# Query and key projection from a split context tile, with the last weighing ahead of the denominator columns

## The chip, the cores and the metric

The kernel runs on one core of one Trainium2 chip. The metric is the device time in microseconds of one execution over the whole input; lower is better. All inputs lie in the chip's memory at the start, and the output is written there.

## The reference

The input `x` holds 32 batches of 128 rows and 1024 columns; `ctx_4096` (the context) has the same shape. Four layers follow each other, each added to x. `_layernorm` is over the last axis.

```python
x = x + _L0_xattn_ref(_layernorm(x), ctx, ...)   # attention over the 1024 columns
x = x + _L0_ffn_ref(_layernorm(x), ...)          # routed product with sign(weight)
x = x + _L1_xattn_ref(_layernorm(x), ctx, ...)   # attention over the 128 context rows
x = x + _L1_ffn_ref(_layernorm(x), ...)          # routed low-rank product
```

The change touches the first layer. There C = 128, T = 1024 and the width of queries and keys is 64:

```python
q = jnp.einsum('dc,bct->btd', Wq, init) + bq     # init is the context
k = jnp.einsum('dc,bct->bdt', Wk, init) + bk[None, :, None]
R = jnp.einsum('btd,bds->bts', q, k)
attention = jax.nn.softmax(R, axis=-1)
v = jnp.einsum('oc,bct->bto', Wv, x) + bv
out = jnp.einsum('bts,bsc->bct', attention, v)
```

## The kernel before

**Trips.** After a set-up block that loads and prepares the weights, all engines run the function `body(k, prepare, attend, chain)` for k = 0 to 33 (`iterations`, L634). Trip k works on three batches at once: it prepares batch b = k (projection, transposed context, values), attends batch a = k - 1 (the first layer's attention over 1024 x 1024 scores) and runs the chain of the three other layers on batch c = k - 2. Trips 2 to 31 do all three; they are the steady state. Trips 0 and 1 lack the later stages, and trips 32 and 33 do not prepare.

**Order.** Every engine has its instructions in a hand-written order, and semaphores tie the engines together. Nothing is reordered by a scheduler: an engine that waits holds up all that stands behind it. SyncE issues the DMAs.

**Two kinds of matmul.** Tiles of type F32 are multiplied in full precision; the hardware records show two matmuls for each such product. Tiles of type F32R hold rounded values, and the records show one matmul each. To keep precision with rounded operands the kernel splits many tiles into a rounded part (`_hi`) and the rest (`_lo`), and adds three products: hi with hi, lo with hi, hi with lo.

**The inner loop.** In each trip the loop over s = 0 to 7 makes one block of scores ahead (`key_scores`), takes the exponent on ScalarE (`prob`), rounds it on ScalarE (`p_hi`), forms the rest on VectorE (`p_lo`), adds to the sum on VectorE (`p_sum`), and multiplies with the values on TensorE (`weigh_values`, six rounded matmuls into `acc`). Steps of the chain are laid in between.

**Its last step, s = 7, on TensorE.** First come the two products of the third layer's attention, `att` half 1 into `shared[1]` (L1338) and half 0 into `shared[0]` (L1340), with `attnT` and `c_val` in full precision. Then the projection of the next batch (L1345): `wqkT`, which holds both weights, times the context tile `c_in`, two halves of 512 columns, into `scores[0]`. Then the sums of the denominators with narrow matmuls (L1352), the eight transposes of `c_in` into `shared` (L1144), and `denominator_columns` (L1221), two transposes of `den_wide`. Then `weigh_values` for s = 7. After the loop eight transposes of `den_inv` (L1372) follow, the transposes of `xn_3` (L1144, the tile is called `p_sum` in the rows since it shares its memory), the values (L1150) and the low-rank product (L1396).

**What VectorE does beside it.** Behind `p_lo` and `p_sum` of s = 6 it writes `kwT` half 0 (`keys_turned`, L932), the reciprocal `r_inv` (L1047), and `p_lo` of s = 7 (L1010). Then it adds the two att halves to `res` (L1052), half 1 first, takes the statistics of `res` (L867 to L875), copies `den_wide` (L906), forms the rest of q (L1068, half 0), the reciprocal `den_inv` (L911), the rest of q (half 1), and `cT_lo` in two halves (L1076). The reciprocal waits for `denominator_columns` on TensorE. The `xn_3` transposes reuse `shared`, half by half, and so wait for the matching half of `cT_lo`; the `c_in` transposes reuse it too, and wait for both halves of `res`.

**What ScalarE does beside it.** It evicts q and k from the projection (L822, L824), then `cT_hi` (L831, L833), `xn_3` (L737) and the denominators (L743).

## Time and profile before

| | before |
|---|---|
| median of 3 runs | 2154.66 us (2151.1 to 2155.81) |
| profiled execution | 2152.07 us |
| its span, first to last instruction | 2150.1 us |
| TensorE matmul busy | 2123.1 us, 99% |
| TensorE weight load busy | 1667.2 us, 78% |
| VectorE busy | 1852.7 us, 86% |
| ScalarE busy | 1160.4 us, 54% |
| mean granted TensorE clock | 0.997 of full speed |

The times of the table are medians of separate executions; the profile is one more execution, 2.6 us below the median. The busy share of an engine says how full it is, not whether another waits for it. The ends of matmuls are modelled, so consecutive matmul rows overlap; the distance from one start to the next (the pitch) is what an instruction costs. The rows of the weight load (PEld) show short waits that the matmul rows hide. For VectorE and ScalarE too, the pitch is a little shorter than the duration of a row.

### The profile page before, as it was taken

The numbers are of one execution on the slowest core, as the hardware profiler recorded it, in microseconds if no ns is written. First come the engines' busy times: TensorE is split into PE (matmuls) and PEld (weight loads), VectorE is DVE, ScalarE is ACT, GpSimd is POOL, SyncE is SP. The second block draws the span as 40 slices with busy tenths as digits, with TensorE's granted clock in tenths as the row PEclk, the third lists the DMA queues.
The fourth block names the chain that finished last, engine by engine and source line by source line (L and its number), as shares of the span: only waits on it lengthen the run. The fifth ranks groups of instructions, "written<-read, shape, count | busy, mean of one in ns | idle before, by whom it ended". The sixth has DMA issues, their size and how long they took to land.

```text
span 2150.1 us, 35721 instructions
## 1 busy us (share of the span) xinstructions
PE 2123.1 (99%) x11503; PEld 1667.2 (78%) x11503; DVE 1852.7 (86%) x3098; ACT 1160.4 (54%) x1721; POOL 264.2 (12%) x306
## 2 busy tenths in 40 slices
PE   9989999999999999999999999999999999999998
PEld 7867777777877777787777777877777787777777
DVE  8268899988888998888899988888998888898984
ACT  4145555655555556555555665555556555555651
POOL 0010111111111111111111111111111111111100
PEclk9999999999999999999999999999999999999999
DMA  6454443233343333334343233343333334343210
GB/s 217 143 157 128 126 129 110 89 113 127 127 137 117 124 100 96 128 118 137 122 131 108 88 117 127 127 137 117 123 97 97 127 122 137 119 135 105 90 50 30
DMA packets 110874, 254.03 MB, mean 118 GB/s; under 512 B 12976, under 2 KB 14272, under 8 KB 110848
## 3 DMA queue, kind: packets, MB, share of 16 engines
q1 hardware_dynamic: 110848, 253.69, 36.8%
q8 instruction: 16, 0.26, 0.1%
q14 instruction: 10, 0.08, 0.0%
HBM read 215.89 MB, written 20.97 MB: 110 GB/s over the span
## 4 chain that ended last, share of the span: by engine, by line
PE 92%; DVE 1%; ACT 1%; issue 1%; POOL 0%; DVEq 0%; POOLq 0%; ACTq 0%
PE acc L1215 17%; PE shared L1144 7%; PE scores L1164 6%; PE acc L1175 6%; PE shared L1189 6%; PE acc L1178 6%; PE acc L1176 6%; PE shared L1190 6%; PE scores L1204 5%; PE scores L1203 5%; PE shared L1396 3%; PE shared L1322 3%; PE scores L1150 3%; PE scores L1345 3%; PE scores L1352 1%; PE shared L1263 1%
## 5 line engine op out<-in xcount | busy, mean ns | idle before, releaser
L1010 DVE TENSOR_TENSOR p_lo<-prob,p_hi 128x1024 fp32r<-128x1024 f32 x256 | 312.3, 1220 | 103.7 <-ACT p_hi L800 85.9
L793 ACT ACTIVATE prob<-scores 128x1024 f32<-128x1024 f32 x256 | 260.7, 1018 | 236.7 <-PE scores L1204 185.5
L885 DVE TENSOR_REDUCE neg_max<-scores 128x1 f32<-128x1024 f32 x256 | 306.9, 1220 | 42.0 <-PE scores L1164 35.1
L704 POOL TENSOR_TENSOR rstd<-var_eps,minus_half 128x1 f32<-128x1 f32 x128 | 126.9, 991 | 1739.9 <-DVE var_eps L875 1739.9
L800 ACT ACTIVATE p_hi<-prob 128x1024 fp32r<-128x1024 f32 x256 | 271.2, 1059 | 42.7 <-PE acc L1215 38.5
L1175 PE MATMUL acc<-m_hi,cT_hi 128*128 128x512 f32 x512 | 217.6, 425 | 0.9 <-DVE x L919 0.9
L1189 PE MATMUL shared<-signT,y_hi 128*128 128x512 f32 x512 | 204.4, 399 | 0.0
L1203 PE MATMUL scores<-q_hl,k_hh 128*128 128x512 f32 x512 | 201.5, 394 | 1.9 <-DVE q_m L992 1.5
L1178 PE MATMUL acc<-m_ring,cT_hi 128*128 128x512 f32 x512 | 203.2, 397 | 0.0
L1176 PE MATMUL acc<-m_hi,cT_lo 128*128 128x512 f32 x512 | 202.5, 396 | 0.0
L1204 PE MATMUL scores<-q_m,k_l 128*128 128x512 f32 x512 | 202.2, 395 | 0.0
L1190 PE MATMUL shared<-signT,y_lo 128*128 128x512 f32 x512 | 201.8, 394 | 0.0
L1018 DVE TENSOR_TENSOR p_sum<-p_sum,prob 128x1024 f32<-128x1024 f32 x160 | 195.0, 1219 | 0.0
L1215 PE MATMUL acc<-p_hi,v_hi 128*128 128x512 f32 x512 | 170.8, 415 | 4.4 <-DVE p_lo L1010 3.9
L1164 PE MATMUL scores<-k_hh,q_hl 128*128 128x512 f32 x512 | 165.2, 404 | 0.3 <-issue 0.3
L1215 PE MATMUL acc<-p_hi,v_lo 128*128 128x512 f32 x512 | 160.9, 395 | 0.0
L1215 PE MATMUL acc<-p_lo,v_hi 128*128 128x512 f32 x512 | 160.8, 395 | 0.0
L1203 PEld LDWEIGHTS scores<-q_hl,k_hh 128*128 128x128 f32 x512 | 96.1, 188 | 25.7 <-issue 1.6
L1164 PEld LDWEIGHTS scores<-k_hh,q_hl 128*128 128x128 f32 x512 | 91.5, 188 | 31.1 <-issue 7.0
L1178 PEld LDWEIGHTS acc<-m_ring,cT_hi 128*128 128x128 f32 x512 | 96.4, 188 | 23.1
L1215 PEld LDWEIGHTS acc<-p_lo,v_hi 128*128 128x128 f32 x512 | 96.0, 188 | 23.4
L1204 PEld LDWEIGHTS scores<-q_m,k_l 128*128 128x128 f32 x512 | 96.1, 188 | 23.1
(222 smaller groups left out, 4214.3 us busy)
## 6 DMA issues: line engine op xcount, KB each, us to landing
m_ring<-m_low SPq DMA_DIRECT2D x512, 256.0 KB, 3.1
c_in<-in_ctx SPq DMA_DIRECT2D x32, 512.0 KB, 3.4
xn<-in_x SPq DMA_DIRECT2D x32, 512.0 KB, 4.2
x<-in_x SPq DMA_DIRECT2D x32, 512.0 KB, 3.3
c_val<-in_ctx SPq DMA_DIRECT2D x32, 512.0 KB, 3.8
out_x<-oscale SPq DMA_DIRECT2D x32, 512.0 KB, 3.0
q_m<-q_hl SPq DMA_DIRECT2D x32, 256.0 KB, 3.1
k_hh<-k_hh SPq DMA_DIRECT2D x32, 256.0 KB, 3.5
```

The lines of the kernel that those rows point to most:

```text
L800: nc.scalar.activation(p_hi[s % 2][:, :], prob[s % 2][:, :], ACT.Identity).then_inc(p_hi_ready, 1)
L885: nc.vector.tensor_reduce(neg_max[:, t:t + 1], scores[t % 2][:, :], AX_X, ALU.max, negate=True).then_inc(row_max, 1)
L1010: nc.vector.tensor_tensor(p_lo[s % 2][:, :], prob[s % 2][:, :], p_hi[s % 2][:, :].bitcast(F32), ALU.subtract).then_inc(p_lo_ready, 1)
L1164: last = mm(scores[t % 2][:, half(h)], q_hl[:, t * P:(t + 1) * P], k_hh[:, half(h)], start=True, stop=True)
L1175: mm(acc[:, half(h)], cT_hi[:, f, :], m_hi[:, f, half(h)], start=f == 0, stop=False)
L1176: mm(acc[:, half(h)], cT_lo[:, f, :], m_hi[:, f, half(h)], start=False, stop=False)
L1178: mm(acc[:, half(h)], cT_hi[:, f, :], m_ring[:, u % SLOTS, :], start=False, stop=f == T - 1).then_inc(kw_unit_done, 1)
L1189: mm(shared[h][:, :], y_hi[:, f, :], signT[:, f, half(h)], start=f == 0, stop=False)
L1190: last = mm(shared[h][:, :], y_lo[:, f, :], signT[:, f, half(h)], start=False, stop=f == T - 1)
L1203: mm(scores[s % 2][:, half(h)], k_hh[:, s * P:(s + 1) * P], q_hl[:, half(h)], start=True, stop=False)
L1204: last = mm(scores[s % 2][:, half(h)], k_l1[:, s * P:(s + 1) * P], q_m[:, half(h)], start=False, stop=True)
L1215: last = mm(acc[:, half(h)], v[:, s, :], p[s % 2][:, half(h)], start=first, stop=end)
```

## The change

The projection's weights are split at set-up into `wqk_hi` and `wqk_lo`. In each trip that prepares, ScalarE rounds the context tile into `c_hi` (behind `p_hi` of s = 4), and VectorE writes the rest, `c_lo` (behind `p_sum` of s = 6 and ahead of `kwT` half 0). TensorE makes six rounded matmuls of 512 columns in place of two full-precision ones: hi with `c_hi` and lo with `c_hi` for both halves, then hi with `c_lo` for both. They stand between att half 1 and att half 0. `denominator_columns` moves behind the last `weigh_values`. `c_hi` takes the memory of `oscale`, `c_lo` is the tile `q_hl` (under that name in the listings), and `attnT` shares its memory with `lowT_lo`, which gives ScalarE one more semaphore to look at (`out_done` of the trip before).

```diff
-        wqkT = sb("wqkT", [P, P])
+        wqk_hi = sb("wqk_hi", [P, P], F32R)
+        wqk_lo = sb("wqk_lo", [P, P], F32R)
...
-                            nc.vector.tensor_copy(wqkT[:, :], s[:, 0:P])
-                            last = nc.vector.tensor_copy(wvT[:, :], s[:, P:2 * P])
+                            nc.vector.tensor_copy(wqk_hi[:, :], s[:, 0:P]).then_inc(b_hi_made, 1)
+                            nc.vector.tensor_copy(wvT[:, :], s[:, P:2 * P])
+                            dve.wait_ge(b_hi_made, 1)
+                            last = nc.vector.tensor_tensor(wqk_lo[:, :], s[:, 0:P], wqk_hi[:, :].bitcast(F32), ALU.subtract)
...
+        c_hi = sb("c_hi", [P, D], F32R)
+        c_lo = q_hl
...
+                        if prepare and s == 4:
+                            act.wait_ge(c_loaded, nth(16, b, 16))
+                            act.wait_ge(xnT_done[2], nth(2, c, 2))
+                            nc.scalar.activation(c_hi[:, :], c_in[:, :], ACT.Identity).then_inc(c_hi_ready, 1)
...
+                            act.wait_ge(out_done, nth(2, c - 1, 2))
...
+                        if prepare and s == 6:
+                            dve.wait_ge(c_hi_ready, nth(1, b, 1))
+                            dve.wait_ge(scores_done, nth(8, a, 8))
+                            nc.vector.tensor_tensor(c_lo[:, :], c_in[:, :], c_hi[:, :].bitcast(F32),
+                                                    ALU.subtract).then_inc(c_lo_ready, 1)
...
+                        if prepare and s == 7:
+                            pe.wait_ge(c_hi_ready, nth(1, b, 1))
+                            pe.wait_ge(exp_ready, nth(8, a, 7))
+                            for h in range(2):
+                                mm(scores[0][:, half(h)], wqk_hi[:, :], c_hi[:, half(h)], start=True, stop=False)
+                                mm(scores[0][:, half(h)], wqk_lo[:, :], c_hi[:, half(h)], start=False, stop=False)
+                            pe.wait_ge(c_lo_ready, nth(1, b, 1))
+                            for h in range(2):
+                                mm(scores[0][:, half(h)], wqk_hi[:, :], c_lo[:, half(h)], start=False, stop=True).then_inc(qk_done, 1)
+                        if chain and s == 7:
                             pe.wait_ge(kwT_ready, nth(2, a, 2))
                             mm(shared[0][:, :], attnT[:, :], c_val[:, half(0)], start=True, stop=True).then_inc(att_done, 1)
-                        if prepare and s == 7:
-                            pe.wait_ge(c_loaded, nth(16, b, 16))
-                            pe.wait_ge(exp_ready, nth(8, a, 7))
-                            for h in range(2):
-                                mm(scores[0][:, half(h)], wqkT[:, :], c_in[:, half(h)], start=True, stop=True).then_inc(qk_done, 1)
...
-                        if attend and s == 7 and prepare:
-                            denominator_columns(a)
                         if attend:
                             weigh_values(a, s)
-                        if attend and s == 7 and not prepare:
+                        if attend and s == 7:
                             denominator_columns(a)
```

The order of TensorE's instructions in the steady trip, from the att products to the transposes of `den_inv`. Before:

```order
L1338 MATMUL shared1<-c_val,attnT 128x512
L1340 MATMUL shared0<-c_val,attnT 128x512
L1345 MATMUL scores0<-c_in,wqkT 128x512 x2
...
L1144 MATMUL shared1<-ident,c_in 128x128 x4
L1221 MATMUL scores1<-ident,xnT 128x128 x2
L1215 MATMUL acc<-p_hi1,v_hi 128x512 x2
L1215 MATMUL acc<-p_hi1,v_lo 128x512 x2
L1215 MATMUL acc<-p_lo1,v_hi 128x512 x2
L1372 MATMUL scores1<-ident,den_inv 128x128 x8
```

After:

```order
L1357 MATMUL shared1<-c_val,attnT 128x512
L1362 MATMUL scores0<-c_hi,wqk_hi 128x512
L1363 MATMUL scores0<-c_hi,wqk_lo 128x512
...
L1366 MATMUL scores0<-q_hl,wqk_hi 128x512 x2
L1369 MATMUL shared0<-c_val,attnT 128x512
...
L1163 MATMUL shared1<-ident,c_in 128x128 x4
L1234 MATMUL acc<-p_hi1,v_hi 128x512 x2
L1234 MATMUL acc<-p_hi1,v_lo 128x512 x2
L1234 MATMUL acc<-p_lo1,v_hi 128x512 x2
L1240 MATMUL scores1<-ident,xnT 128x128 x2
L1394 MATMUL scores1<-ident,den_inv 128x128 x8
```

The projection, now six instructions, stands ahead of att half 0, and the two transposes of `den_wide` (called `xnT`, whose memory it shares) stand behind the weighing.

VectorE in the same trip, from the last `p_sum` to the first addition to `res`. Before:

```order
L1018 TENSOR_TENSOR p_sum<-p_sum,prob0 128x1024
L932 TENSOR_TENSOR kwT<-shared0,key_bias 128x512
L1047 RECIPROCAL r_inv1<-r_sum1 128x1
L1010 TENSOR_TENSOR p_lo1<-prob1,p_hi1 128x1024
L1052 SCALAR_TENSOR_TENSOR res<-shared1,r_inv1,res 128x512
L1052 SCALAR_TENSOR_TENSOR res<-shared0,r_inv1,res 128x512
```

After, where `q_hl<-c_in,c_hi` is `c_lo`:

```order
L1032 TENSOR_TENSOR p_sum<-p_sum,prob0 128x1024
L1060 TENSOR_TENSOR q_hl<-c_in,c_hi 128x1024
L946 TENSOR_TENSOR kwT<-shared0,key_bias 128x512
L1066 RECIPROCAL r_inv1<-r_sum1 128x1
L1024 TENSOR_TENSOR p_lo1<-prob1,p_hi1 128x1024
L1071 SCALAR_TENSOR_TENSOR res<-shared1,r_inv1,res 128x512
L1071 SCALAR_TENSOR_TENSOR res<-shared0,r_inv1,res 128x512
```

One subtraction of 1024 columns is added in front of `kwT` half 0; the rest keeps its order.

ScalarE in the same trip, at s = 4 and 5, before:

```order
L748 ACTIVATE xnT<-shared0 128x512
L800 ACTIVATE p_hi0<-prob0 128x1024
L793 ACTIVATE prob1<-scores1 128x1024
L800 ACTIVATE p_hi1<-prob1 128x1024
```

After:

```order
L757 ACTIVATE xnT<-shared0 128x512
L809 ACTIVATE p_hi0<-prob0 128x1024
L816 ACTIVATE c_hi<-c_in 128x1024
L802 ACTIVATE prob1<-scores1 128x1024
L809 ACTIVATE p_hi1<-prob1 128x1024
```

The conversion of the context tile stands between `p_hi` of s = 4 and the exponent of s = 5.

## Rows read from the trace of the kernel before

**Rows 1.** The page, busy time by engine: share of the span, number of instructions.

```profile
PE 2123.1 (99%) x11503; PEld 1667.2 (78%) x11503; DVE 1852.7 (86%) x3098; ACT 1160.4 (54%) x1721; POOL 264.2 (12%) x306
```

**Rows 2.** Waits of TensorE in the whole span: total us, times, longest.

```profile
PE acc L1215 <- DVE p_lo L1010: 3.9, 5, 1.2
```

**Rows 3.** Line L1076 (VectorE, cT_lo): its operations and who waited for it.

```profile
L1076 DVE TENSOR_TENSOR cT_lo<-shared,cT_hi x64: 681/686/693, 121.4 to 2031.0; 128x512 fp32r<-128x512 f32 x64
...
  PEld shared L1144: 5.2, 29
```

**Rows 4.** TensorE in order of time, steady state: start us, us, what, count.

```profile
1029.53 0.63 PE L1215 MATMUL acc<-p_lo,v_hi 128*128 128x512 f32 x2
1030.00 1.02 PE L1338 MATMUL shared<-c_val,attnT 128*128 128x512 f32 x2
1030.86 1.02 PE L1340 MATMUL shared<-c_val,attnT 128*128 128x512 f32 x2
1031.71 1.88 PE L1345 MATMUL scores<-c_in,wqkT 128*128 128x512 f32 x4
1033.52 0.64 PE L1352 MATMUL scores<-p_sum,ones 128*32 128x256 f32 x8
...
1034.53 1.09 PE L1144 MATMUL shared<-ident,c_in 128*128 128x128 f32 x8
...
1037.20 1.03 PE L1372 MATMUL scores<-ident,den_inv 128*128 128x128 f32 x8
1038.08 1.22 PE L1144 MATMUL shared<-ident,p_sum 128*128 128x128 f32 x8
```

**Rows 5.** VectorE in order of time, same stretch; in brackets idle before it.

```profile
1029.43 0.68 DVE L932 TENSOR_TENSOR kwT<-shared,key_bias 128x512 f32<-128x512 f32 x1
1030.03 0.15 DVE L1047 RECIPROCAL r_inv<-r_sum 128x1 f32<-128x1 f32 x1
1030.77 1.23 DVE L1010 TENSOR_TENSOR p_lo<-prob,p_hi 128x1024 fp32r<-128x1024 f32 x1 [0.59 <-DVE r_inv L1047]
1031.91 1.40 DVE L1052 SCALAR_TENSOR_TENSOR res<-shared,r_inv,res 128x512 f32<-128x512 f32 x2
1033.35 0.69 DVE L867 BATCH_NORM_STATS2 stat<-res 128x6 f32<-128x512 f32 x1
...
1035.05 0.42 DVE L906 COPY xnT<-scores 128x256 f32<-128x256 f32 x1
...
1036.28 0.21 DVE L911 RECIPROCAL den_inv<-scores 128x8 f32<-128x8 f32 x1
1036.52 0.74 DVE L1068 SCALAR_TENSOR_TENSOR q_hl<-scores,bqk_col,q_hl 64x512 fp32r<-64x512 f32 x1
1037.30 1.29 DVE L1076 TENSOR_TENSOR cT_lo<-shared,cT_hi 128x512 fp32r<-128x512 f32 x2
1038.82 0.69 DVE L918 TENSOR_TENSOR prob<-acc,prob 128x512 f32<-128x512 f32 x1 [0.23 <-ACT prob L743]
```

**Rows 6.** ScalarE in order of time, same stretch.

```profile
1024.20 1.03 ACT L793 ACTIVATE prob<-scores 128x1024 f32<-128x1024 f32 x1 [1.51 <-DVE p_sum L1018]
...
1029.62 1.06 ACT L800 ACTIVATE p_hi<-prob 128x1024 fp32r<-128x1024 f32 x1
```

**Rows 7.** TensorE, the same projection one trip later.

```profile
1093.76 1.88 PE L1345 MATMUL scores<-c_in,wqkT 128*128 128x512 f32 x4
```

**Rows 8.** All engines at the first trip, in order of time.

```profile
115.50 1.95 PE L1345 MATMUL scores<-c_in,wqkT 128*128 128x512 f32 x4 [1.46 <-PEq L189]
...
116.63 0.68 ACT L822 ACTIVATE q_hl<-scores,bqk_col 64x512 fp32r<-64x512 f32 x1 [1.59 <-PE scores L1345]
...
117.05 0.15 DVE L875 TENSOR_TENSOR var_eps<-mean_var,var_eps 128x1 f32<-128x1 f32 x1
```

**Rows 9.** VectorE at the second trip, the last p_lo, no idle before it.

```profile
165.21 1.22 DVE L1010 TENSOR_TENSOR p_lo<-prob,p_hi 128x1024 fp32r<-128x1024 f32 x1
```

**Rows 10.** Window with PE busy, PEld, DVE, ACT, POOL, then granted clock, DMA.

```profile
123.00:126.00 3.00, 3.00 (x10) 2.43 (x10) 2.40 (x4) 0.60 (x1) 0.00 (x0) 0.58 0.87 182
```

More of the change, by code:

```diff
@@ L340, in _ @@
                             nc.vector.tensor_copy(hi, turned).then_inc(b_hi_made, 1)
-                            dve.wait_ge(b_hi_made, i + 1)
+                            dve.wait_ge(b_hi_made, i + 2)
                             last = nc.vector.tensor_tensor(lo, turned, hi.bitcast(F32), ALU.subtract)
@@ L486, in build @@
         den_wide = xnT[:, 0:2, :].rearrange("p t c -> p (t c)")
-        oscale = sb("oscale", [P, D])
+        with ExitStack() as before:
+            oscale = sb("oscale", [P, D], F32, before)
+        c_hi = sb("c_hi", [P, D], F32R)
+        c_lo = q_hl
         c_val = sb("c_val", [P, D])
@@ L510, in build @@
         gate_parts = attn
-        attnT = sb("attnT", [P, P])
+        with ExitStack() as before:
+            attnT = sb("attnT", [P, P], F32, before)
         low = attn
+        lowT_lo = sb("lowT_lo", [P, P], F32R)
         lowT_hi = sb("lowT_hi", [P, P], F32R)
-        lowT_lo = sb("lowT_lo", [P, P], F32R)
         def psum(name, shape):
@@ L535, in build @@
         qk_done = sem("qk_done")
+        c_hi_ready = sem("c_hi_ready")
+        c_lo_ready = sem("c_lo_ready")
         doubled = sem("doubled")
```

## The prediction

> **What bounds the kernel now.** I read the busy times first: TensorE is busy for 99% of the span, VectorE for 86%, ScalarE for 54% [rows 1]. The longest wait of TensorE's matrix half inside the trips is small: 3.9 us in five places together [rows 2]. One trip over a batch takes 62.05 us, from one projection to the next [rows 4, 7]. That looks like a kernel in which TensorE alone counts. So I asked next who feeds TensorE just in time. The line that writes cT_lo on VectorE answers it: TensorE's weight loads of the transposes waited for it 29 times, 5.2 us in all, or 0.18 us each, and there are 30 full trips [rows 3]. These waits are short enough to vanish in the busy share. In the timeline the second cT_lo ends at 1037.30 + 1.29 = 1038.59, and the eight transposes of xn_3 (called p_sum there) that need it take 1.06 us, from 1038.08 to the values at 1039.14, where eight transposes of den_inv took 0.88 [rows 4, 5]. So VectorE arrives at this point no earlier than TensorE does. Followed backwards, VectorE has no idle mark from cT_lo at 1037.30 to the last p_lo at 1030.77: res, statistics, den_wide, q_hl, den_inv and q_hl stand one behind another. The only slack is 0.59 us, before that last p_lo [rows 5]. The second bound is thus a VectorE chain of 7.8 us that begins right where the change adds work.
>
> **TensorE's own work.** Removed: four f32 records of the projection. Their pitch is 0.43 (1030.00 to 1030.86 holds two), together 1.71; the further 0.10 up to 1033.52 belongs to the step to the narrow matmuls of L1352, which stays. Added: six rounded matmuls of 512 columns. Two of these take 1030.00 - 1029.53 = 0.47, so six take 1.41 [rows 4]. The gain is 0.3 us a trip, 9.6 us over 32, if nothing else counts. One more change between f32 and rounded operands could cost 0 to 0.1; I take 0.
>
> The trace shows an f32 product as two records of 0.43, 3.7 times one rounded matmul of 0.235 [rows 4]. The Trainium skill ("FP8 and Floating Point Precision", TensorE Precision Notes) says that true FP32 makes four passes through the array. By that rule three products save a quarter of 1.71, or 0.43 a trip and 13.7 us in all; by the rows it is 0.3 and 9.6.
>
> **ScalarE.** Added per trip: one conversion of 128x1024, c_hi, like p_hi at 1.06 us, behind the fifth p_hi. The next long idle of ScalarE is 1.51 us before the seventh exp (1024.20), where it waits for VectorE [rows 6]. The conversion fits into it, so I cost it at nothing; if that cover were gone, the price would be 1.06 less the slack of whoever waits. The context tile was loaded long before, behind the previous products.
>
> **VectorE.** Added per trip: one subtraction of 128x1024, c_lo, like p_lo, whose pitch is 1.14 (1030.77 to 1031.91) [rows 5]. It stands between the last p_sum and the first half of kwT. Worked on from there: c_lo at 1029.43, kwT at 1030.57, r_inv at 1031.17 to 1031.32, the last p_lo at 1031.35 instead of 1030.77. So 1.14 is added and 0.59 of idle absorbs half: **+0.58**. The p_hi that it needs has been ready since 1030.68 [rows 6], so there is no more to absorb.
>
> **The products in front of att(0).** The att product for half 0 used to follow half 1 directly; now the six matmuls stand between. Half 1 ends at 1030.86, the products at 1032.27 (c_lo is ready at 1030.65, no wait), att(0) at 1033.12 by pitch, with its last result at 1033.29. VectorE could take res half 0 at 1033.15 (32.57 + 0.58) and gets it at about 1033.34, with 0.05 for the hand-off: another **+0.17**. The transposes of c_in on TensorE need that res: it is ready at 1034.1, TensorE arrives at 33.21 + 1.01 = 1034.22. That just fits, with 0.1 to spare [rows 4, 5].
>
> **The weighing in front of the columns.** Before, the two den_wide transposes stood ahead of the six matmuls of the last weighing, which hid the round trip to VectorE's den_inv. Now: transposes of c_in until 1035.22, weighing until 1036.63, columns, whose result lies in PSUM at 1036.63 + 0.17 + 0.27 = 1037.07. The reciprocal would be due at 1036.28 + 0.75 = 1037.03 and starts at 1037.11: **+0.08**. den_wide itself is ready in time (35.05 + 0.75 + 0.42 = 1036.22). TensorE meanwhile rests from 1036.85 to about 1037.37, for the den_inv transposes. This is where its 0.3 us and more goes: it runs ahead and then stands [rows 4, 5].
>
> **Sum for one trip.** The chain is later by 0.58 + 0.17 + 0.08 = 0.83. cT_lo ends at 1039.42 instead of 1038.59, and the second half of the xn_3 transposes, hence all that follows on TensorE, is later by **0.83 us**. TensorE's gain of 0.3 is not subtracted: it lies ahead of this wait. Nothing later gives it back, since TensorE is full and its order fixed. Behind this point VectorE idles 0.23 before prob [rows 5], so its own steps there move by 0.6 only and are not late for a TensorE that moved by 0.83. Bounds: with the 0.1 of the weighing's fit lost and 0.1 for a change of operand kind twice, 1.1; if res half 0 and the columns cost nothing, 0.58. Thirty trips have all three stages: 24.9 us (17 to 33).
>
> **First two trips.** At the first, nothing covers the split. Before, the first eviction of q starts at 116.63. Now VectorE ends its statistics at 117.20, c_lo takes until 118.4, one more matmul with its latency 0.45: about 118.9, so +2.2, and TensorE already waits behind ScalarE there [rows 8]. At the second there is no chain and no idle before the last p_lo [rows 9]; the 1.14 comes through but for a little: +1.0. The last two trips have no projection, and their order is unchanged. The small operation that forms wqk_lo falls into the set-up, beside TensorE's long products: nothing.
>
> **Result.** 24.9 + 2.2 + 1.0 = 28.1 us. On the profiled execution (span 2150.1, time 2152.07) that is 2180.2; on the median of the runs, 2154.66, it is 2182.8. I take 2181.5, between the two.
>
> **Rivals.** (1) Faster: TensorE alone sets the pace and the VectorE delay is covered. Then 32 times -0.3 and +2.2 at the start: 2147. It needs a chain that comes no later than now at the cT_lo point. For it speaks the 99%; against it the 29 waits [rows 3]. Chance 0.06. The page's four passes, named above, would make it 2143. (2) The chain moves by a fraction only, because VectorE's idle times before 1029 are larger than I read and c_lo starts earlier: 0.25 a trip, 7.5 + 3.2, or 2165. The split is bound to its place behind p_sum, so 0.08. (3) ScalarE joins: the conversion makes the sixth exp and p_hi late, or the shifted statistics make the evictions of den_rows the last to come: 0.45 a trip more, 2195. The 1.51 of idle speaks against it for the first part, the 0.23 of VectorE before prob bounds the second. Chance 0.08. (4) The granted clock falls. After the long rests of the first trip, the window from 123 to 126 us had 0.58 [rows 10], so some of it at 1.2 GHz: about 1.3 us lost. With the same in every trip 39 us more: 2221. The new rests are half a microsecond each between full work, so 0.03. The forecast keeps 0.75.
>
> **Range and chances.** The forecast's own bounds are 2154.66 + 20 to 2154.66 + 36, so 2172 to 2191, with 2 us for the spread of runs. To hold 8 in 10 I take in part of rival 2: 2167 to 2192. A measurement here can tell about 0.2%, or 4.3 us, from no change. Faster by more: 0.06. Within: 0.04, the lower edge of rival 2. Slower: 0.90.
>
> **What would show it.** In the new profile the trip should last 62.9 us. Waits of TensorE should appear at den_inv (about 0.5 us, for VectorE's reciprocal) and at the xn_3 transposes for cT_lo (about 0.5 and more), once a trip. The idle of 0.59 before VectorE's last p_lo must be gone. ScalarE must keep an idle before the seventh exp, of about 0.5. If the trip lasts 61.8, rival 1 holds; if TensorE waits for p_lo or for x3, my slacks in the middle were read too wide.

## The result and the profile after

The changed kernel takes 2176.39 us (median of 4 runs, 2176.22 to 2176.71); the kernel before, run beside it, 2153.98 us (median of 4 runs, 2151.1 to 2155.81). The ratio is 1.0106, with a 95% interval of 1.0094 to 1.0118: 22.4 us slower. The forecast was 2181.5, with a range of 2167 to 2192. The profiled execution has a span of 2174.1 us, 24.0 more than before.

The page of the changed kernel, busy time by engine, beside [rows 1]:

```profile
PE 2121.5 (98%) x11567; PEld 1679.3 (77%) x11567; DVE 1890.0 (87%) x3131; ACT 1193.5 (55%) x1753; POOL 264.8 (12%) x306
```

TensorE is busy for 1.6 us less, VectorE for 37 us more (32 times `c_lo`), ScalarE for 33 us more (32 times `c_hi`). These sums do not show the loss. The waits of TensorE do (us in total, times, longest), beside [rows 2]:

```profile
PE shared L1163 <- DVE cT_lo L1095: 12.5, 30, 0.5
PE scores L1394 <- DVE den_inv L925: 11.9, 32, 0.5
PE acc L1234 <- DVE p_lo L1024: 3.0, 4, 1.3
```

Once in each trip TensorE now waits for `den_inv`, and once for `cT_lo`, 0.4 us each. The 3 us behind `p_lo` were there before. The view of the `cT_lo` line (L1095) says the same for the weight loads, beside [rows 3]:

```profile
  PEld shared L1163: 24.1, 58
  PE shared L1163: 12.5, 30
```

From 29 waits of 0.18 us before, it has gone to 58 of 0.42. One of the two in each trip stands before the second half of the `xn_3` transposes, where the 29 of before stood; the other stands before their first half, which before had none.

Now the same stretch of a steady trip as in [rows 5], VectorE of the changed kernel (start us, us, what, idle before it). To compare with before, subtract 14.08 us: that is where TensorE begins the att product of half 1 in both.

```profile
1043.52 1.22 DVE L1060 TENSOR_TENSOR q_hl<-c_in,c_hi 128x1024 fp32r<-128x1024 f32 x1
1044.65 0.69 DVE L946 TENSOR_TENSOR kwT<-shared,key_bias 128x512 f32<-128x512 f32 x1
1045.25 0.16 DVE L1066 RECIPROCAL r_inv<-r_sum 128x1 f32<-128x1 f32 x1
1045.45 1.23 DVE L1024 TENSOR_TENSOR p_lo<-prob,p_hi 128x1024 fp32r<-128x1024 f32 x1
1046.59 1.53 DVE L1071 SCALAR_TENSOR_TENSOR res<-shared,r_inv,res 128x512 f32<-128x512 f32 x2
1048.16 0.69 DVE L881 BATCH_NORM_STATS2 stat<-res 128x6 f32<-128x512 f32 x1
...
1051.09 0.21 DVE L925 RECIPROCAL den_inv<-scores 128x8 f32<-128x8 f32 x1
...
1052.10 1.29 DVE L1095 TENSOR_TENSOR cT_lo<-shared,cT_hi 128x512 fp32r<-128x512 f32 x2
1053.31 0.68 DVE L932 TENSOR_TENSOR prob<-acc,prob 128x512 f32<-128x512 f32 x1
```

`c_lo` is the row `q_hl<-c_in,c_hi`. The last `p_lo` starts at 1045.45, or 1031.37 on the clock of before, against 1030.77: later by 0.60, and the idle in brackets is gone. The statistics of `res` start at 1034.08 against 1033.35: 0.73. The reciprocal `den_inv` starts at 1037.01 against 1036.28, and `cT_lo` at 1038.02 against 1037.30: still 0.73 and 0.72. The delay of 0.72 that `cT_lo` has is the delay of the trip, to 0.02.

The two additions to `res` take 1.53 us together, against 1.40: the second starts 0.81 after the first instead of 0.66. It starts just behind the end of TensorE's att product of half 0 (1046.32 + 1.02 = 1047.34, below), so that of the two late paths TensorE's is the last one at this point, by 0.15 us.

TensorE in the same stretch, beside [rows 4]:

```profile
1044.08 1.02 PE L1357 MATMUL shared<-c_val,attnT 128*128 128x512 f32 x2
1044.53 0.79 PE L1362 MATMUL scores<-c_hi,wqk_hi 128*128 128x512 f32 x1
...
1045.86 0.62 PE L1366 MATMUL scores<-q_hl,wqk_hi 128*128 128x512 f32 x2
1046.32 1.02 PE L1369 MATMUL shared<-c_val,attnT 128*128 128x512 f32 x2
...
1048.27 1.09 PE L1163 MATMUL shared<-ident,c_in 128*128 128x128 f32 x8
...
1050.60 0.38 PE L1240 MATMUL scores<-ident,xnT 128*128 128x128 f32 x2
1051.35 1.09 PE L1394 MATMUL scores<-ident,den_inv 128*128 128x128 f32 x8 [0.37 <-DVE den_inv L925]
1052.85 1.25 PE L1163 MATMUL shared<-ident,p_sum 128*128 128x128 f32 x8 [0.41 <-DVE cT_lo L1095]
1053.94 0.50 PE L1169 MATMUL scores<-wvT,xn 128*128 128x128 f32 x3
```

The six rounded products take 1.38 us, from 1044.94 (1044.08 plus two records of 0.43) to 1046.32; `q_hl` as an operand of L1366 is `c_lo`. TensorE reaches the transposes of `c_in` at 1034.19 on the clock of before, 0.34 earlier than it did. It runs ahead, then idles 0.37 before `den_inv` and 0.41 before the `xn_3` transposes, and starts the values at 1053.94, or 1039.86 against 1039.14: 0.72 late. From the values of one trip to those of the next it is 62.81 us in the mean of the 29 steady distances, against 62.07 before: 0.74 more.

ScalarE hides its new work. The seventh exponent and the last `p_hi`:

```profile
1038.30 1.03 ACT L802 ACTIVATE prob<-scores 128x1024 f32<-128x1024 f32 x1 [0.58 <-DVE p_sum L1032]
...
1043.72 1.06 ACT L809 ACTIVATE p_hi<-prob 128x1024 fp32r<-128x1024 f32 x1
```

Its idle before the seventh exponent has shrunk from 1.51 to 0.58 us [rows 6]. The last `p_hi` starts at 1029.64 on the clock of before, against 1029.62.

At the first trip nothing covers the split, beside [rows 8]:

```profile
115.69 1.06 ACT L816 ACTIVATE c_hi<-c_in 128x1024 fp32r<-128x1024 f32 x1 [0.66 <-PEq L190]
...
117.10 1.22 DVE L1060 TENSOR_TENSOR q_hl<-c_in,c_hi 128x1024 fp32r<-128x1024 f32 x1
...
118.91 0.68 ACT L836 ACTIVATE q_hl<-scores,bqk_col 64x512 fp32r<-64x512 f32 x1 [2.17 <-PE scores L1366]
```

The first eviction of q starts at 118.91 against 116.63, 2.28 us later, and so do TensorE's values of this trip (123.03 against 120.76).

### The profile page after: what moved, and what is told of

Read it like the earlier page. It is cut to its first block, busy times and chain, and to the rows that moved or that the text cites. A ratio compares the mean times of both kernels' runs of the same rounds, so it can differ in the third digit from the quotient of the medians.

```text
span 2174.1 us, 36007 instructions
## 1 busy us (share of the span) xinstructions
PE 2121.5 (98%) x11567; PEld 1679.3 (77%) x11567; DVE 1890.0 (87%) x3131; ACT 1193.5 (55%) x1753; POOL 264.8 (12%) x306
## 4 chain that ended last, share of the span: by engine, by line
PE 84%; DVE 8%; issue 2%; ACT 1%; POOL 0%; DVEq 0%; POOLq 0%; ACTq 0%
PE acc L1234 14%; PE shared L1163 6%; PE scores L1183 6%; PE acc L1194 6%; PE shared L1208 6%; PE acc L1197 6%; PE acc L1195 6%; PE shared L1209 5%; PE scores L1223 5%; PE scores L1222 5%; PE shared L1418 3%; PE scores L1169 3%; PE shared L1341 3%; DVE q_hl L1087 2%; PE shared L1282 1%
```

## The experiments

"Trip" is the distance from the values of one trip to those of the next, the mean over the steady trips of the profiled execution; the ratio is against the kernel before, run beside it on the same chip (medians of 2151.99 to 2153.98). f1 and f2 leave the values of one of the three products out of the projection; the amount of TensorE's work is the same.

| kernel | median us | ratio (95%) | trip us |
|---|---|---|---|
| before | 2153.98 | 1 | 62.07 |
| changed | 2176.39 | 1.0106 (1.0094 to 1.0118) | 62.81 |
| e1 split alone | 2173.79 | 1.0094 (1.0078 to 1.0111) | 62.67 |
| e2 columns late alone | 2183.58 | 1.0142 (1.0125 to 1.0159) | 63.07 |
| e3 changed, columns back | 2176.80 | 1.0113 (1.0096 to 1.0129) | 62.81 |
| e4 changed, att back | 2193.57 | 1.0184 (1.0167 to 1.0201) | 63.30 |
| e5 changed, c_lo on GpSimd | 2253.03 | 1.0466 (1.0445 to 1.0486) | 65.22 |
| e6 as e5, att back | 2249.28 | 1.0446 (1.0429 to 1.0463) | 65.09 |
| e7 as e6, columns back | 2240.77 | 1.0407 (1.0389 to 1.0424) | 64.86 |
| e8 conversion alone | 2152.44 | 0.9999 (0.9990 to 1.0009) | 62.06 |
| f1 changed, no c_lo | 2175.15 | 1.0098 (1.0083 to 1.0113) | 62.79 |
| f2 as f1, att and columns back | 2160.44 | 1.0035 (1.0026 to 1.0045) | 62.29 |
| f3 before, normalization later | 2151.95 | 0.9994 (0.9986 to 1.0003) | 62.00 |
| f4 work moved to ScalarE | 2162.56 | 1.0045 (1.0032 to 1.0058) | 62.31 |

The theory at the start was the VectorE chain from the last `p_lo` to `cT_lo`. The rivals were TensorE's own work, the conversion on ScalarE, and costs of the three edits that simply add up.

### e1: the split alone

To the kernel before, with its full-precision projection:

```diff
...
+                            nc.scalar.activation(c_hi[:, :], c_in[:, :], ACT.Identity).then_inc(c_hi_ready, 1)
...
+                            nc.vector.tensor_tensor(c_lo[:, :], c_in[:, :], c_hi[:, :].bitcast(F32),
+                                                    ALU.subtract).then_inc(c_lo_ready, 1)
...
                             pe.wait_ge(c_loaded, nth(16, b, 16))
+                            pe.wait_ge(c_lo_ready, nth(1, b, 1))
```

> The kernel before, with the split of the context tile alone: ScalarE writes c_hi, VectorE writes c_lo at the new place, the full-precision projection stays and only waits for c_lo. Theory (a VectorE chain from the last p_lo to cT_lo sets the trip, and 0.59 us of idle absorbs half of the 1.14): the trip goes from 62.07 to 62.65, with 3 us more at the start about 2174 us. Rival (TensorE's own work sets the trip, the split is hidden): 62.07 a trip and about 2157 us. If the whole 1.14 came through: 63.2 and about 2191.

VectorE in the steady trip:

```profile
1042.07 1.22 DVE L1055 TENSOR_TENSOR q_hl<-c_in,c_hi 128x1024 fp32r<-128x1024 f32 x1
...
1043.99 1.23 DVE L1019 TENSOR_TENSOR p_lo<-prob,p_hi 128x1024 fp32r<-128x1024 f32 x1
1045.14 1.41 DVE L1066 SCALAR_TENSOR_TENSOR res<-shared,r_inv,res 128x512 f32<-128x512 f32 x2
...
1049.51 0.21 DVE L920 RECIPROCAL den_inv<-scores 128x8 f32<-128x8 f32 x1
...
1052.04 0.69 DVE L927 TENSOR_TENSOR prob<-acc,prob 128x512 f32<-128x512 f32 x1 [0.23 <-ACT prob L748]
```

Measured: 62.67 a trip and 2173.79 us. From the last `p_lo` to `den_inv` it is 5.52 us, against 5.51 before, and TensorE's att half 1 starts at 1042.64 here, so that the last `p_lo` stands 1.35 behind it against 0.77: the 0.58. The split alone costs 0.60 a trip, against 0.74 for the whole change, and half of the subtraction's 1.14 us is absorbed. The rival of TensorE's own work falls: TensorE's matmuls are the same as before.

### e8: the conversion alone

```diff
...
+                            nc.scalar.activation(c_hi[:, :], c_in[:, :], ACT.Identity).then_inc(c_hi_ready, 1)
...
                             pe.wait_ge(c_loaded, nth(16, b, 16))
+                            pe.wait_ge(c_hi_ready, nth(1, b, 1))
```

> The kernel before with the conversion c_hi on ScalarE alone, which the projection waits for but does not use. Theory: hidden in ScalarE's idle of 1.51 us, 62.07 a trip, 1 us more at the start, about 2155 us. Rival (ScalarE joins the chain): up to 1.06 a trip, 2187 us.

Measured: 62.06 a trip, ratio 0.9999. The conversion on ScalarE costs nothing that can be measured, in the kernel before. In the changed kernel ScalarE keeps 0.58 us of idle before the seventh exponent, so that rival falls there too.

### e2: the columns behind the last weighing, alone

```diff
-                        if attend and s == 7 and prepare:
-                            denominator_columns(a)
                         if attend:
                             weigh_values(a, s)
-                        if attend and s == 7 and not prepare:
+                        if attend and s == 7:
                             denominator_columns(a)
```

> The kernel before, with the last weighing ahead of the denominator columns and nothing else. Theory of three parallel paths: the columns' result lies in PSUM at 1037.4 instead of before 1036.3, so den_inv and all behind it on VectorE are later by 1.1: a trip of 63.2 us, about 2188 us. The recorded prediction's sum, which gave this step 0.08 on top of the others, would make it 62.15 and 2157. Rival (the round trip to VectorE hides behind the transposes that follow): no change, 2154.

VectorE in the steady trip, the last `p_lo` and `den_inv`:

```profile
1045.15 1.23 DVE L1010 TENSOR_TENSOR p_lo<-prob,p_hi 128x1024 fp32r<-128x1024 f32 x1 [0.59 <-DVE r_inv L1047]
...
1051.64 0.21 DVE L911 RECIPROCAL den_inv<-scores 128x8 f32<-128x8 f32 x1 [1.01 <-PE scores L1221]
```

The idle of 0.59 before `p_lo` is as before; a new idle of 1.01 stands before the reciprocal, which waits for the columns (L1221). The trip grows by 1.00 and the time by 30.8 us against the 2152.74 us that the kernel before took beside it. This edit alone costs more than the whole change. The recorded sum had given it 0.08, but on top of a VectorE that is 0.75 late by then; alone it is 1.0.

### e3: the changed kernel with the columns back

```diff
+                        if attend and s == 7 and prepare:
+                            denominator_columns(a)
                         if attend:
                             weigh_values(a, s)
-                        if attend and s == 7:
+                        if attend and s == 7 and not prepare:
                             denominator_columns(a)
```

> The changed kernel with the denominator columns back ahead of the last weighing. Theory: no change, 62.8 a trip and 2176 us, since the additions to res are late on VectorE anyway and den_inv is not reached earlier. Rival (the order of the columns carries the loss, since TensorE now waits about 0.5 us for den_inv in each trip): 62.3 a trip and 2160.

TensorE's wait for `den_wide` (the tile is called `xnT`) in this kernel:

```profile
PE scores L1240 <- DVE xnT L920: 29.3, 30, 1.0
```

Measured: 62.81 a trip, the same as the changed kernel to 0.01. TensorE now idles 1 us in one place, before the columns, instead of 0.4 in two. The order of the columns is not what costs in the changed kernel, and putting it back gives nothing. In the kernel before, in which `res` was not late, it cost 1.0 (e2).

### e4: the changed kernel with att half 0 back

```diff
                             mm(shared[1][:, :], attnT[:, :], c_val[:, half(1)], start=True, stop=True).then_inc(att_done, 1)
+                            pe.wait_ge(kwT_ready, nth(2, a, 2))
+                            mm(shared[0][:, :], attnT[:, :], c_val[:, half(0)], start=True, stop=True).then_inc(att_done, 1)
...
-                        if chain and s == 7:
-                            pe.wait_ge(kwT_ready, nth(2, a, 2))
-                            mm(shared[0][:, :], attnT[:, :], c_val[:, half(0)], start=True, stop=True).then_inc(att_done, 1)
```

> The changed kernel with att half 0 back in front of the projection. The recorded sum (0.14 of the loss from this step, costs that add up): 62.65 a trip, 2172 us. Parallel paths: VectorE reaches res earlier, but den_inv then waits for the columns at 1036.9, so the trip is 62.73 and the time 2174. Rival (the late product carries the loss): 62.1 and 2155.

Both expectations missed: 63.30 a trip, 2193.57 us. TensorE's att half 0, and VectorE's `den_inv`:

```profile
1050.57 1.13 PE L1359 MATMUL shared<-c_val,attnT 128*128 128x512 f32 x2 [0.28 <-DVE kwT L946]
```

```profile
1056.77 0.21 DVE L925 RECIPROCAL den_inv<-scores 128x8 f32<-128x8 f32 x1 [0.67 <-PE scores L1240]
```

att half 0 is written to `shared[0]`, which VectorE must have read for `kwT` first, and `kwT` now stands behind `c_lo` on VectorE. TensorE is free at 1049.28 + 0.86 = 1050.14, and starts att half 0 at 1050.57: 0.43 late, with the whole projection and all else behind it. The columns, which stand behind the weighing here as in e2, then come later still, and VectorE idles 0.67 before `den_inv`. The products between the att halves in the changed kernel thus cover a delay that `c_lo` itself makes. e1 shows the same wait (8.5 us in 30 trips); there VectorE comes to `res` later still, and has no idle from its last `p_lo` to `den_inv`.

### f1: the changed kernel without c_lo

```diff
...
-                            nc.vector.tensor_tensor(c_lo[:, :], c_in[:, :], c_hi[:, :].bitcast(F32),
-                                                    ALU.subtract).then_inc(c_lo_ready, 1)
...
-                            pe.wait_ge(c_lo_ready, nth(1, b, 1))
                             for h in range(2):
-                                mm(scores[0][:, half(h)], wqk_hi[:, :], c_lo[:, half(h)], start=False, stop=True).then_inc(qk_done, 1)
+                                mm(scores[0][:, half(h)], wqk_hi[:, :], c_hi[:, half(h)], start=False, stop=True).then_inc(qk_done, 1)
```

> The changed kernel without c_lo: VectorE does not form it, and the third rounded product reads c_hi in its place, so TensorE's work and order are the same (that product's values are left out of the projection). Costs that add up: the trip falls from 62.81 to 62.25, about 2159 us. Parallel paths: att half 0 ends at the same moment, res half 0 and all behind it stay where they are: 62.8 a trip and about 2174 us, only the first trip gaining 1 to 2 us.

VectorE in the steady trip:

```profile
1045.42 1.23 DVE L1024 TENSOR_TENSOR p_lo<-prob,p_hi 128x1024 fp32r<-128x1024 f32 x1 [0.59 <-DVE r_inv L1061]
...
1047.94 0.75 DVE L1066 SCALAR_TENSOR_TENSOR res<-shared,r_inv,res 128x512 f32<-128x512 f32 x1 [0.64 <-PE shared L1363]
...
1051.66 0.21 DVE L925 RECIPROCAL den_inv<-scores 128x8 f32<-128x8 f32 x1
```

Measured: 62.79 a trip and 2175.15 us. The suspected cost is taken away, and 0.02 comes back. The idle of 0.59 before `p_lo` has returned, so `res` half 1 is on time, but `res` half 0 now waits 0.64 for TensorE's late att product (L1363), and from there on VectorE stands where it stands in the changed kernel. This decides between costs that add up (62.25) and parallel paths (62.8) for the latter. The columns are still behind the weighing here, but VectorE has no idle before `den_inv`, so it is the att product that ends last.

### f2: all three undone

As f1, and the edits of e3 and e4 as well.

> As the run without c_lo (the third product reads c_hi), with att half 0 back in front of the projection and the columns back ahead of the weighing. Theory: the VectorE chain is that of the kernel before, 62.07 a trip and, with 1 to 2 us at the start, about 2155 us; the 0.3 us that TensorE saves does not show. Rival (TensorE's work counts): 61.8 a trip, 2147. Rival (rounded products or the conversion cost something of their own): 62.3 or more, above 2160.

Trip 62.29, 2160.44 us: 0.22 above the expected 62.07. VectorE, then TensorE's columns, then ScalarE's first eviction of q:

```profile
1038.94 1.22 DVE L1024 TENSOR_TENSOR p_lo<-prob,p_hi 128x1024 fp32r<-128x1024 f32 x1 [0.59 <-DVE r_inv L1061]
...
1044.45 0.21 DVE L925 RECIPROCAL den_inv<-scores 128x8 f32<-128x8 f32 x1
...
1047.26 0.69 DVE L932 TENSOR_TENSOR prob<-acc,prob 128x512 f32<-128x512 f32 x1 [0.50 <-ACT prob L752]
```

```profile
1043.70 0.44 PE L1235 MATMUL scores<-ident,xnT 128*128 128x128 f32 x2 [0.28 <-DVE xnT L920]
```

```profile
1041.21 0.68 ACT L836 ACTIVATE q_hl<-scores,bqk_col 64x512 fp32r<-64x512 f32 x1 [2.36 <-PE scores L1362]
```

The VectorE chain is that of before: 0.59 of idle, and 5.51 us from `p_lo` to `den_inv`. TensorE comes to the columns 0.28 too early and waits for `den_wide`, which is where its saved time goes. The 0.22 comes from another place. The kernel makes the products with `wqk_hi` and `wqk_lo` for both halves first and the third products last, so the first half of the projection is complete 0.3 us later than the full-precision one was. ScalarE begins to evict q 2.27 us after `p_lo` starts, against 2.00 before (1032.77 - 1030.77 by ScalarE's row in the trace of before). It has no idle from there to the denominators, so VectorE waits 0.50 for them instead of 0.23 [rows 5]. TensorE's values still start as in the kernel before, 9.16 us behind att half 1 against 9.15. The loss comes 9.6 us behind the start of the values, at transposes that reuse `shared` and wait for VectorE's `oscale`: the weight loads wait there 16.8 us in all instead of 13.3. This is a second meeting point of VectorE and TensorE in the trip (see f3). In the changed kernel this delay does not exist, since the projection stands earlier there. The rival that rounded products cost something by their kind would give the same 62.3; the trace speaks for their order, and no run without `c_lo` made them half by half.

### e5, e6, e7: c_lo on GpSimd

```diff
...
+                    if prepare and attend:
+                        pool.wait_ge(c_hi_ready, nth(1, b, 1))
+                        pool.wait_ge(scores_done, nth(8, a, 8))
+                        nc.gpsimd.tensor_tensor(c_lo[:, :], c_in[:, :], c_hi[:, :].bitcast(F32),
+                                                ALU.subtract).then_inc(c_lo_ready, 1)
...
-                        if prepare and s == 6:
+                        if prepare and not attend and s == 6:
```

> The changed kernel with c_lo written by GpSimd instead of VectorE from the second trip on (GpSimd takes about 2.4 us for such a tile and is idle there). Costs that add up: 0.58 comes back, 62.25 a trip, 2158 us. Parallel paths: att half 0 still comes late, res half 0 is added at the same moment, and nothing comes back: 62.8 a trip, 2176 us.

> c_lo on GpSimd and att half 0 back in front of the projection; the columns stay behind the weighing. Costs that add up: 62.1 a trip, 2155 us. Parallel paths: the columns alone still hold den_inv until 1036.94 instead of 1036.28, so 62.73 a trip, 2174 us.

> c_lo on GpSimd, att half 0 back in front of the projection, columns back ahead of the weighing; the rounded products stay. Both theories: the VectorE chain is as in the kernel before, 62.07 a trip, and with some 3 us more at the start about 2157 us. TensorE's 0.3 us stays without effect, since cT_lo comes when it did. Rival (something else in the change costs, the conversion on ScalarE or the rounded products, or GpSimd slows VectorE): above 62.3 a trip, 2163 or more. Rival (TensorE's work counts): 61.8, 2148.

All three missed, but for the rival in the last that GpSimd slows VectorE: 65.22, 65.09 and 64.86 a trip. VectorE and GpSimd of e7 at the same moment:

```profile
1069.91 3.40 DVE L1029 TENSOR_TENSOR p_lo<-prob,p_hi 128x1024 fp32r<-128x1024 f32 x1
```

```profile
1069.36 2.87 POOL L730 TENSOR_TENSOR q_hl<-c_in,c_hi 128x1024 fp32r<-128x1024 f32 x1 [2.38 <-PE scores L1228]
```

A `p_lo` that takes 1.22 us elsewhere took 3.40 while GpSimd worked on its subtraction, once in each of 31 trips in all three kernels. GpSimd was done at 1072.23, and the next VectorE row starts 1.01 us later: that fits a VectorE that stood still until then, and `p_lo` of s = 6, on which TensorE and ScalarE hang, came 2.2 us late. The Trainium skill ("SBUF — State Buffer", SBUF: two separate sides) says that the two engines share a port pair, which whichever starts first holds for the whole instruction, when VectorE reads two operands from SBUF and the GpSimd instruction reads SBUF too. The trace agrees. A smaller part of the loss is the granted clock: its mean is 0.991 to 0.995 in these profiles, and the median steady trip of e7 is 64.54 where the mean is 64.86. These three kernels therefore say nothing on the three edits; f1 and f2 replaced them.

### f3: the kernel before with more slack in the chain

```diff
...
-                        if prepare and attend and s == 6:
-                            normalize(0, b, xn, xn)
...
+                    if prepare and attend:
+                        normalize(0, b, xn, xn)
```

> The kernel before with one ScalarE step moved: the normalization of the next batch's x stands behind the last p_hi instead of between the seventh and the eighth exponent. The last p_hi comes about 0.3 us earlier and VectorE's chain with it. Theory (cT_lo is already as late as TensorE before the change): TensorE gains the 0.1 us that it waits for cT_lo, 61.97 a trip, about 3 us in all, 2150. Rival (TensorE alone sets the pace): no change, 62.07.

The trip falls from 62.07 to 62.00, and no wait of TensorE for `cT_lo` is left in the trace. The time, 0.9994 (0.9986 to 1.0003), can't be told from no change.

The last `p_hi` comes 0.25 us earlier, and the idle before the last `p_lo` shrinks from 0.59 to 0.35: it is `p_hi` that `p_lo` waits for, though the brackets name `r_inv`. `cT_lo` and TensorE's values come 0.24 earlier as well, so VectorE's chain was the later of the two already in the kernel before, by at least that much at the values. But the trip gains only 0.07. VectorE's next step waits longer for ScalarE's denominators, and TensorE loses the rest at the second meeting point (the weight loads of before, then of f3):

```profile
1040.40 0.69 DVE L918 TENSOR_TENSOR prob<-acc,prob 128x512 f32<-128x512 f32 x1 [0.47 <-ACT prob L743]
```

```profile
PEld shared L1144 <- DVE oscale L1125: 13.3, 59, 0.2
PEld shared L1144 <- DVE oscale L1125: 16.6, 59, 0.3
```

So two things set the trip: the start of the values, and `prob` on VectorE, which has 0.07 us to spare in the kernel before. Taken from the traces, behind att half 1, the later of the two gives the trips of all kernels but those with `c_lo` on GpSimd, to 0.04 us. In e1 to e4, f1, f4 and the changed kernel it is the values; in f2 and f3 it is `prob`.

### f4: work moved to ScalarE

The changed kernel with att half 0 and the columns back, the three products of a half made together, ScalarE in place of VectorE for two copies (shown), and three other ScalarE steps moved:

```diff
...
+                            if attend:
+                                act.wait_ge(xnT_done[2], nth(2, c, 2))
+                                nc.scalar.activation(tile4(xnT, 1), shared[1][:, :], ACT.Identity).then_inc(xnT_b_ready[2], 1)
...
+                        nc.scalar.activation(den_wide, scores[1][:, 0:2 * P], ACT.Identity).then_inc(den_wide_ready, 1)
```

> A version meant to beat both: the changed kernel with att half 0 and the columns back in front, the products half by half, and VectorE relieved on the chain: the second half of the third layer's transposed tile and den_wide are copied by ScalarE, attnT stands behind the eighth exponent, the normalization of x behind the last p_hi, and the evictions of k behind those of the denominators. The chain should be 0.45 us earlier than in the kernel before although c_lo stands in it, and TensorE's 0.3 us then count: 61.7 to 61.9 a trip, with 2 us at the start 2144 to 2150. If ScalarE's normalization of res becomes the last to come, 62.0 and 2154.

Missed: 62.31 a trip, 2162.56 us (ratio 1.0045). VectorE at `p_lo` of s = 4, and TensorE at att half 0:

```profile
1028.61 1.23 DVE L1039 TENSOR_TENSOR p_lo<-prob,p_hi 128x1024 fp32r<-128x1024 f32 x1 [0.29 <-ACT p_hi L817]
```

```profile
1038.72 1.13 PE L1374 MATMUL shared<-c_val,attnT 128*128 128x512 f32 x2 [0.29 <-DVE kwT L961]
```

VectorE's 0.6 us from the first copy were lost at once: it now waits 0.29 for `p_hi`, which stands behind the copy on ScalarE, and as much again for TensorE's scores of the third layer. `c_lo` thus starts no earlier, `kwT` is late for att half 0 as in e4, and TensorE waits 0.29 there. Of the kernels with the complete rounded projection this is the fastest, but it does not beat the kernel before. No run did, clear of noise.

## Why the prediction was right, and where it was not

**The bound.** That VectorE arrives at `cT_lo` no earlier than TensorE was right, and the 29 waits of the weight load were the sign. e1 shows it from one side (the chain 0.58 later, the trip 0.60 longer) and f3 from the other (the chain and the values 0.24 earlier). What the prediction did not see is the second meeting point 9.6 us on, which leaves only 0.07 of those 0.24.

**TensorE's work.** Predicted 0.3 us a trip saved and lost again in waits; measured 1.38 us for the six products in place of 1.71, and 0.78 us of idle in two places. The waits were forecast as about 0.5 each and are 0.37 and 0.41.

**ScalarE.** Predicted hidden; e8 measured 0.

**VectorE's c_lo.** Predicted +0.58 at the last `p_lo`, measured 0.60, and 0.58 in e1.

**att half 0.** Predicted +0.17 more at the statistics, measured +0.13. The price was right. But it is only what this path has over that of `c_lo`: f1 shows that the late product costs the full 0.7 when `c_lo` is gone. The `c_in` transposes fitted as forecast, at 1034.19 for 1034.22, with nothing to spare: TensorE's matmul rows show no idle there, and the weight loads wait 0.4 us for `res`.

**The columns.** Predicted +0.08, measured 0: TensorE came to the columns at 1036.52 (1050.60 on its own clock) instead of 1036.63, and the reciprocal followed the rest of q on VectorE directly. Again the amount hid a path of its own, worth 1.0 when it stands alone (e2).

**The trip.** Predicted +0.83, measured +0.74; 30 trips make 22.3 instead of 24.9. The columns' 0.08 is nearly all of the difference.

**The first trips.** Predicted +2.2 for the first, measured +2.28. Predicted +1.0 for the second; from the first values to those of trip 2 the distance grew by 2.78 us, 2.0 beyond a steady trip's 0.74. In part that is the granted clock: TensorE rests longer in the first trip, the clock was 0.50 of full speed from 119 to 127 us where it was 0.89 and then 0.69 before, and the sixteen records of the values that took 2.59 us in the kernel before took 3.78.

**The end.** Not predicted: the last 45 us. In the profiled execution of the kernel before the last trip ran at a lower clock for a while; in that of the changed kernel it did not (window, TensorE busy, ..., granted clock, DMA share, GB/s). Before, then after:

```profile
2104.00:2108.00 4.00, 3.29 (x30) 2.27 (x29) 0.37 (x3) 1.72 (x5) 1.74 (x1) 0.65 0.74 257
2108.00:2112.00 4.00, 4.00 (x21) 3.99 (x20) 0.60 (x4) 0.27 (x1) 0.00 (x0) 0.50 0.00 0
```

```profile
2128.00:2132.00 4.00, 2.29 (x20) 1.42 (x19) 1.86 (x3) 1.06 (x3) 2.08 (x1) 1.00 0.36 128
2132.00:2136.00 4.00, 3.54 (x42) 2.95 (x34) 0.98 (x6) 1.05 (x5) 0.46 (x1) 1.00 0.39 138
```

The stretch from the last values to the end is 117.9 us before and 115.2 after. It is not the change: e8, whose last two trips are those of before, has 115.2 as well, and e3 and e4, whose last two trips are those of the changed kernel, have 118.0 and 119.2. So the predicted 28.1 against the span's 24.0 is 2.6 from the size of the trip, 2.7 from this, less 1.1 at the start.

The likeliest case held, and the rivals fell: TensorE alone (e1), a fraction only (e1), ScalarE (e8), and the clock, whose mean was 0.997 in both. That the total, 2181.5 against 2176.39, came so near is in small part luck: the steady trips were forecast 2.6 us too dear in all and the first trips 1.1 too cheap.

No term of the steady trip was wrong by more than 0.1 us; the form of the sum misleads. The moments behind it are worked out rightly, each from whichever path comes last. But its three amounts are not shares that could be won back one by one. They are what each of three paths has over the one before it, and so they say nothing of what a path costs by itself: that is 0.60 us a trip for the split alone (e1), 1.00 for the columns alone (e2), 0.72 for the late product with the columns but without `c_lo` (f1), and 0.74 for all together. The late product entirely by itself was not run, nor was the kernel with both orders put back and `c_lo` still on VectorE, except with other steps moved too (f4, 0.24 above before).

## What to carry to other kernels

Where one engine waits for another by a little, cheaper work on the one that waits gains nothing, and work added to the other costs at once, less the idle in front of it. Taking work off that other engine gains only up to the next meeting point (f3: 0.24 there, 0.07 in the trip). When several edits lengthen parallel paths to the same wait, work out each path by itself and take the latest: undoing one of them may return nothing (e3, f1) or cost more (e4). Look for short waits of the weight load before trusting a TensorE that is 99% busy.

## What the runs showed of the hardware

Rounded matmuls of 512 columns keep their pitch of 0.23 us behind a full-precision one: the six of the projection take 1.38 us between the two att products of the changed kernel. No price for the change of kind was seen.

GpSimd's subtraction of 128x1024 with both operands in SBUF held up VectorE's for 2.2 us of its 2.87 (e7). `res` plus bias on GpSimd (2.40 us), once a trip in the kernel before, does no such harm. VectorE takes its maxima at that time, each from one operand in PSUM: three of them take 3.48 us together, 1.13 by pitch, and none takes over 1.23 us. Whether it is the place of the operand or there being only one that matters, no run here shows.

The granted clock of the last trip differed between executions whose instructions there are the same, and is worth up to 4 us: the last stretch takes 115.2 (e8) to 119.2 (e4).
